# A new order for the steps of 32 batches of Performer attention, head attention and eight experts on one Trainium2 core: pieces of the same tile shape put side by side

## The chip, the cores and the metric
One core of one Trainium2 chip. The time is the device time of one launch in microseconds. Of the kernel before, three runs gave 1332.08, 1335.20 and 1335.43 us; their median, 1335.2 us, is what the changed kernel is held against.

## What is computed
For each of 32 batches, 256 tokens of width 256 (all float32):

```
x = x + tanh(g_xattn) * performer(layernorm(x), ctx, ctx, features)   # 16 heads of 16, 64 features, causal
x = x + tanh(g_ffn) * ffn(layernorm(x))

performer: q, k scaled; q' = exp(q@F) + 1e-4, k' = exp(h_k + k@F - max h_k) + 1e-4
           running sums S += k' v, Z += k'; out = (q' S) / (q' Z)
ffn:       h = rmsnorm(x); q = h@Wq + bq; k, v = ((h@Wdown + bdown)@Wup + bup)
           att = softmax over the 16 heads of one token of q k / 4; out = att v
           x = x + out@Wo + bo
           h2 = rmsnorm(x); gate = softmax(h2@Wg + bg)
           x + sum over 8 experts of gate_e * (h2 @ We_e)
```

## The kernel before
The five engines run hand-written streams in one block, synchronised by semaphores. Every step of a batch is a small function under `@per_batch`, which issues it once for each batch and in order. Each engine has a written-out start (some fifty to a hundred and twenty steps) and then `for n in range(-1, NB + 3): slot(n)`; `slot(n)` is the engine's fixed order in the steady part, and a step's argument (`n - 3` to `n + 1`) is the batch that it works on in this slot. So five batches are in flight. Before its instructions a step waits for the steps of other engines that it needs (`wait_ge(*at("name", batch))`); these waits hold for some ranges of batches only, where an earlier wait of the same engine doesn't already cover them. `Signal` groups steps of an engine on one semaphore, so steps of one group have to come in the order of the group. Eight banks of PSUM are given to the steps by hand in `BANK`.

TensorE's steps, in order of the mathematics, with their tile shapes and, for one batch, the matmul records of the trace (each has one weight load; plain float32 products count twice):

- `keys_turned`, `queries_turned`, `h_tr_`: transposes of the context, of the normed x and of the key norms. 128x128; 4, 4 and 2.
- `fk_`, `fq_`: the random features of keys and queries, rows of 32 (`feature_products`, L1609 and L1616). 20 and 12.
- `X00_`, `X01_`, `X10_`, `X11_`: scores of the first 128 keys against all queries, and `Y0_`, `Y1_`: of the second 128 keys against the second 128 queries. Rows of 64 (L1624, L1632). 8 each and 16 each. ScalarE or VectorE copies them to `att`, GpSimd or VectorE masks them.
- `av0_` to `av3_`: attended values, columns of 32 (L1639). 16 each. `nt_t_` turns the numerators (L1649). 8.
- `hn_turned`, `dn_`, `qq_`, `kv0_`, `kv1_`: the layer-normed x turned, and the projections of the second block. 128x128; 4, 6, 12, 2, 2.
- `s0_` to `s3_`: the head scores of each token, in four pieces (`head_scores`, L1658); `pv0_` to `pv3_`: the head mix, in four pieces (`head_mix`, L1666). Tiles of 32x32, 64 matmuls of 16 columns and 64 loads in each piece. These eight pieces are 512 of a batch's 792 matmuls.
- `o_tr_`, `out_project`, `h2_t0_`, `h2_t1_`, `g_`, `g_t_`: the head output turned, its projection, the second norm turned, the gate. 128x128 but for `g_t_`, which has rows of 8; 4, 12, 2, 2, 6, 2.
- `mm00_` to `mm03_`, `mm10_` to `mm13_`: the experts, two at a time, for the two halves of the tokens (`expert_products`, L1593 to L1595). 128x128, six matmuls of 512 columns each. VectorE adds each result to `z`, weighted by the gate (`a00_` and so on, L1047).

Between `pv3_` and `o_tr_` stand VectorE's `out_tokens` (L1056) and GpSimd's `out_normal` (L395). TensorE's steady order before is:

```
mm01 hn mm02 X00 dn o_tr qq X01 mm03 kv0 c_tr kv1 h_tr o Y0 s0 X10 av0 s1 av1 X11 s2 Y1 mm10
h2_t0 s3 av2 h2_t1 mm11 x_tr av3 fk nt_t g mm12 g_t pv0 fq pv1 mm13 pv2 mm00 pv3
```

(`c_tr` is `keys_turned`, `x_tr` `queries_turned`, `hn` `hn_turned`, `o` `out_project`.) A dense piece is issued like this:

```python
for n in range(32 * part // PARTS, 32 * (part + 1) // PARTS):
    for j in range(4):
        r = slice(32 * j, 32 * j + 32)
        last = pe.matmul(ps[r, BANK["pv"], n:512:32], p_t[r, n, :], v_t[r, :, n],
                         start=True, stop=True, tile_position=(32 * j, 32 * j))
```

Of the kernel before, what the change touches and what calls it, by code (L numbers as in the profile page):

```python
# [5 lines left out]
F32 = mybir.dt.float32  # L6
# [73 lines left out]
def build(nc, x_d, ctx_d, gx_d, gf_d, rf_d, g1_d, wq_d, bq_d, wdn_d, bdn_d, wup_d, bup_d,  # L80
          wo_d, bo_d, g2_d, wg_d, bg_d, we_d, out_d):
    ctx = ExitStack()
    with ctx:
# [94 lines left out]
        with ExitStack() as early:  # L178
# [30 lines left out]
            signal("q_pe", "c_t"),  # L209
            signal("q_pe_b", "h_tr"),  # L210
# [3 lines left out]
            signal("q_dve_c", "k_lo q_lo"),  # L214
            signal("q_act", "h_hi h_t_"),
            signal("q_act_b", "k_hi"),
            signal("q_act_c", "xn q_hi"),
            signal("q_pool", "rstd q_r"),
            signal("r0_pe", "fk fq"),
            signal("r0_act", "ek2 eq3"),  # L220
            signal("r0_act_b", "ek1 eq0 eq2"),
            signal("r0_act_c", "ek3"),
            signal("r0_act_d", "ek0 eq1"),
            signal("r0_pool", "pk2 pk3"),
            signal("r0_pool_b", "pq0 pq3"),
            signal("r0_pool_c", "pk1 pq1 pq2"),
            signal("r0_pool_d", "pk0"),
            signal("p0_pe", "X00 X01 Y0 av0 av1"),
            signal("p0_dve", "y00"),
            signal("p0_dve_b", "y01"),  # L230
            signal("p0_act", "x000 x011 nt0"),
            signal("p0_act_b", "x001 x010"),
            signal("p0_pool", "v1"),
            signal("p0_pool_b", "m00 m01"),
# [3 lines left out]
            signal("p1_act", "x100 x111 nt1"),  # L238
            signal("p1_act_b", "x110"),
            signal("p1_act_c", "x101"),  # L240
            signal("p1_pool", "m10 m11 x1"),
            signal("g_dve", "g_st g_mv g_bn"),
            signal("g_act", "hn y"),
            signal("g_pool", "r_f g_r yb"),
            signal("f_pe", "h_t dn qq kv0 kv1 s3"),
            signal("f_dve", "ht_lo d_lo bqq q_t bkv1 k_t v_t p_t s_sum s_tok ssum"),
            signal("f_dve_b", "bkv0 smax ssub"),
            signal("f_act", "ht_hi d_hi q_bd p_bd s_exp"),
            signal("o_pe", "pv3"),
            signal("o_pe_b", "o_tr o h2_t0 h2_t1"),  # L250
            signal("o_dve", "o_tok ot_lo y2 h2_lo0 h2_lo1"),
            signal("o_act", "ot_hi sq h2n h2_hi0 h2_hi1"),
            signal("o_pool", "o_n ms_e r2"),
            signal("o_pool_b", "z_y z0"),
            signal("e_pe", "g g_t mm00"),
            signal("e_pe_b", "mm01 mm02 mm03 mm10 mm11 mm12 mm13"),
            signal("e_dve", "ga gmax gm gsum grec gate a00_ a00"),
            signal("e_dve_b", "a01_ a01 a02_ a02 a03_ a03 a10_ a10 a11_ a11 a12_ a12 a13_ a13"),
# [31 lines left out]
        def _(sp):  # L290
            @per_batch
            def load_x_(q):
                if 2 <= q <= 4:
                    sp.wait_ge(*at("x1", q - 2))
                sp.dma_start(x_in[q % 2][:, :, :], rows(x_d, q)).then_inc(*x_load.up(q))
# [39 lines left out]
            for n in range(-1, NB + 3):  # L335
                slot(n)
# [6 lines left out]
        def _(pool):  # L343
# [3 lines left out]
            @per_batch  # L347
            def pk2_(q):
                if q in (0, 1) or q >= 3:
                    pool.wait_ge(*at("ek2", q))  # L350
                pool.tensor_scalar(pairs(kf, q, 2), pairs(kf, q, 2), KERNEL_EPS, 1.0, ALU.add, ALU.mult).then_inc(*up("pk2", q))

            @per_batch
            def values(p):
                if not p:
                    pool.wait_ge(*w_dve.at("v1_one"))
                pool.tensor_copy(v1[:, :, :, 0:HD], c_in[p % 2][:, :, :].rearrange("p t (h d) -> p t h d", d=HD)).then_inc(*up("v1", p))

            @per_batch
            def g_r_(g):  # L360
                pool.wait_ge(*at("g_bn", g))
# [7 lines left out]
            @per_batch  # L369
            def pq0_(q):  # L370
                if q in (0,) or q >= 3:
                    pool.wait_ge(*at("eq0", q))
                pool.tensor_scalar(pairs(qf, q, 0), pairs(qf, q, 0), KERNEL_EPS, 1.0, ALU.add, ALU.mult).then_inc(*up("pq0", q))  # L373

            @per_batch
            def pk1_(q):
                if q in (0, 2):
                    pool.wait_ge(*at("ek1", q))
                pool.tensor_scalar(pairs(kf, q, 1), pairs(kf, q, 1), KERNEL_EPS, 1.0, ALU.add, ALU.mult).then_inc(*up("pk1", q))

            @per_batch
            def pk0_(q):
                if q <= 1:
                    pool.wait_ge(*at("ek0", q))
                pool.tensor_scalar(pairs(kf, q, 0), pairs(kf, q, 0), KERNEL_EPS, 1.0, ALU.add, ALU.mult).then_inc(*up("pk0", q))

            @per_batch
            def pq1_(q):
                pool.wait_ge(*at("eq1", q))
                pool.tensor_scalar(pairs(qf, q, 1), pairs(qf, q, 1), KERNEL_EPS, 1.0, ALU.add, ALU.mult).then_inc(*up("pq1", q))  # L390
# [7 lines left out]
            @per_batch  # L398
            def pk3_(q):
                if not q:  # L400
                    pool.wait_ge(*at("ek3", q))
                pool.tensor_scalar(pairs(kf, q, 3), pairs(kf, q, 3), KERNEL_EPS, 1.0, ALU.add, ALU.mult).then_inc(*up("pk3", q))

            @per_batch
            def pq3_(q):
                if q <= 2:
                    pool.wait_ge(*at("eq3", q))
                pool.tensor_scalar(pairs(qf, q, 3), pairs(qf, q, 3), KERNEL_EPS, 1.0, ALU.add, ALU.mult).then_inc(*up("pq3", q))

            @per_batch  # L410
            def pq2_(q):
                if q in (0,) or q >= 2:
                    pool.wait_ge(*at("eq2", q))
                pool.tensor_scalar(pairs(qf, q, 2), pairs(qf, q, 2), KERNEL_EPS, 1.0, ALU.add, ALU.mult).then_inc(*up("pq2", q))

            @per_batch
            def m00_(p):
                if not p:
                    pool.wait_ge(*at("x000", p))
                if p:  # L420
                    pool.wait_ge(*at("x010", p))
                pool.affine_select(out=att[:, 0, :, 0:P], in_=att[:, 0, :, 0:P], compare_op=ALU.is_ge, fill=0.0, base=0,
                                   pattern=[[0, 4], [1, P]], channel_multiplier=-1).then_inc(*up("m00", p))

            @per_batch
            def m01_(p):
                if p <= 1:
                    pool.wait_ge(*at("x011", p))
# [1711 lines left out]
```

## Time and profile before

| | |
|---|---|
| runs | 1332.08, 1335.20, 1335.43 us; median 1335.2 |
| profiled execution | 1344.52 us |
| its span | 1342.8 us, 55815 instructions |
| mean granted clock of TensorE in it | 0.982 of 2.4 GHz |
| busy: TensorE, VectorE, ScalarE, GpSimd | 93%, 70%, 56%, 42% |

The profiled execution is one run by itself, so shares and durations are compared within it. TensorE's row counts matmuls; its weight loads run beside them and have a row of their own, `PEld`. In the waits and in the chain "issue" is time in which an engine stood and no semaphore explains it. The granted clock is 1.00 at 2.4 GHz and 0.50 at 1.2 GHz.

### The profile page before, as it was taken

The numbers are of one execution on the slowest core, as the hardware profiler recorded it, in microseconds if no ns is written. First come the engines' busy times: TensorE is split into PE (matmuls) and PEld (weight loads), VectorE is DVE, ScalarE is ACT, GpSimd is POOL, SyncE is SP. The second block draws the span as 40 slices with busy tenths as digits, with TensorE's granted clock in tenths as the row PEclk, the third lists the DMA queues.
The fourth block names the chain that finished last, engine by engine and source line by source line (L and its number), as shares of the span: only waits on it lengthen the run. The fifth ranks groups of instructions, "written<-read, shape, count | busy, mean of one in ns | idle before, by whom it ended". The sixth has DMA issues, their size and how long they took to land.

```text
span 1342.8 us, 55815 instructions
## 1 busy us (share of the span) xinstructions
PE 1255.5 (93%) x25344; PEld 975.1 (73%) x25344; DVE 936.9 (70%) x2166; ACT 755.1 (56%) x1502; POOL 559.2 (42%) x873
## 2 busy tenths in 40 slices
PE   0568999999999999999999999999999999999997
PEld 0347777777777777777777777777777777777775
DVE  5465677677777677766777777777777777777665
ACT  5366655565555565654556556555665555566431
POOL 0254345343434443443444444454444434444421
PEclk9987999999999999998999999999999999999999
DMA  8300000000000000000000000000000000000000
GB/s 283 106 18 18 19 26 26 27 3 26 27 26 26 27 18 11 26 27 26 26 27 8 21 26 27 26 26 27 26 2 27 26 26 26 27 26 3 10 19 16
DMA packets 40221, 40.72 MB, mean 30 GB/s; under 512 B 4144, under 2 KB 39728, under 8 KB 39984
## 3 DMA queue, kind: packets, MB, share of 16 engines
q1 hardware_dynamic: 38896, 37.11, 8.9%
q8 instruction: 199, 3.26, 1.0%
q14 instruction: 38, 0.31, 0.1%
q10 hardware_dynamic: 1088, 0.04, 0.1%
HBM read 28.75 MB, written 8.39 MB: 28 GB/s over the span
## 4 chain that ended last, share of the span: by engine, by line
PE 92%; DVE 3%; issue 2%; POOL 1%; DMA 1%; SPq 1%; ACT 1%; DVEq 0%
PE ps L1593 15%; PE ps L1595 12%; PE ps L1594 12%; PE ps L1624 10%; PE ps L1639 8%; PE ps L1666 7%; PE ps L1658 6%; PE ps L1632 5%; PE ps L1587 4%; PE ps L1609 4%; PE ps L1649 3%; DVE hk L1367 1%; PE ps L1875 1%; DMA x_in<-in_x 1%; SPq L319 1%
## 5 line engine op out<-in xcount | busy, mean ns | idle before, releaser
L1047 DVE SCALAR_TENSOR_TENSOR z<-ps,gate,z 128x256 f32<-128x256 f32 x512 | 247.4, 483 | 143.8 <-PE ps L1595 133.3
L1593 PE MATMUL ps<-we_hi,h_hi 128*128 128x512 f32 x512 | 226.2, 442 | 3.3 <-issue 1.2
L1595 PE MATMUL ps<-we_hi,h_lo 128*128 128x512 f32 x512 | 204.9, 400 | 0.0
L1594 PE MATMUL ps<-we_lo,h_hi 128*128 128x512 f32 x512 | 204.1, 399 | 0.0
L1624 PE MATMUL ps<-qf,kf 64*128 64x256 f32 x1024 | 148.9, 410 | 4.0 <-POOL qf L373 4.0
L1593 PEld LDWEIGHTS ps<-we_hi,h_hi 128*128 128x128 f32 x512 | 97.6, 191 | 33.4 <-issue 12.2
L1666 PEld LDWEIGHTS ps<-v_t,p_t 32*32 32x32 f32 x8192 | 84.3, 107 | 48.7 <-issue 47.8
L495 POOL TENSOR_TENSOR x<-o_x,x_in 128x512 f32<-128x512 f32 x32 | 41.1, 1285 | 188.3 <-DVE o_x L1274 188.3
L1624 PEld LDWEIGHTS ps<-qf,kf 64*128 64x128 f32 x1024 | 90.5, 190 | 34.4 <-issue 23.0
L1595 PEld LDWEIGHTS ps<-we_hi,h_lo 128*128 128x128 f32 x512 | 97.9, 191 | 23.2
L1639 PE MATMUL ps<-att,v 128*32 128x256 f32 (+1 forms) x2048 | 111.9, 334 | 1.2 <-DVE att L1205 0.6
L1666 PE MATMUL ps<-v_t,p_t 32*32 32x16 f32 x8192 | 98.8, 186 | 13.2 <-issue 13.1
L1594 PEld LDWEIGHTS ps<-we_lo,h_hi 128*128 128x128 f32 x512 | 98.4, 192 | 12.4 <-issue 0.3
L1658 PEld LDWEIGHTS ps<-k_t,q_bd 32*32 32x32 f32 x8192 | 81.3, 105 | 28.5 <-issue 23.4
L435 POOL TENSOR_SCALAR ms_e<-ms 128x2 f32<-128x2 f32 x32 | 6.1, 191 | 227.5 <-ACT h2n L696 227.5
L1658 PE MATMUL ps<-k_t,q_bd 32*32 32x16 f32 x8192 | 94.3, 185 | 2.8 <-issue 2.0
L1196 DVE TENSOR_TENSOR att<-ps,causal 128x512 f32<-128x512 f32 x32 | 22.1, 691 | 97.0 <-PE ps L1632 97.0
L1639 PEld LDWEIGHTS ps<-att,v 128*32 128x32 f32 x2048 | 54.8, 109 | 43.0 <-issue 17.7
L615 ACT ACTIVATE ht_hi<-ps 128x512 fp32r<-128x512 f32 x32 | 19.2, 599 | 116.5 <-PE ps L1587 116.5
L659 ACT ACTIVATE q_bd<-q_t,sel_tok 128x512 f32<-128x512 f32 x64 | 76.6, 1254 | 2.7 <-DVE q_t L1113 2.7
L395 POOL TENSOR_TENSOR o_n<-o_tok,s_rec 128x512 f32<-128x512 f32 x32 | 41.6, 1300 | 85.6 <-DVE o_tok L1056 85.5
L1632 PE MATMUL ps<-qf,kf 64*128 64x128 f32 x1024 | 74.9, 284 | 1.3 <-issue 1.2
(210 smaller groups left out, 3076.4 us busy)
## 6 DMA issues: line engine op xcount, KB each, us to landing
x_in<-in_x SPq DMA_DIRECT2D x32, 256.0 KB, 3.5
c_in<-in_ctx SPq DMA_DIRECT2D x32, 256.0 KB, 3.2
c_chunk<-in_ctx SPq DMA_DIRECT2D x16, 512.0 KB, 7.4
out<-z SPq DMA_DIRECT2D x32, 256.0 KB, 2.6
stage<-in_L_ffn_We SPq DMA_DIRECT2D x2, 1024.0 KB, 9.8
stage_q<-in_L_ffn_Wq SPq DMA_DIRECT2D x1, 256.0 KB, 6.4
stage_u<-in_L_ffn_Wup SPq DMA_DIRECT2D x2, 128.0 KB, 5.4
stage_b<-in_L_ffn_bup SPq DMA_DIRECT2D x1, 256.0 KB, 6.6
```

The lines of the kernel that those rows point to most:

```text
L659: last = act.activation(q_bd[:, :, t, :], q_t[:, :, :].rearrange("p h n -> p n h"), ACT.Copy, scale=sel_tok[:, t:t + 1])
L1047: return dve.scalar_tensor_tensor(out=z[e % 2][:, t, :], in0=ps[:, bank, ex % 2 * D:(ex % 2 + 1) * D], scalar=gate[:, t, ex:ex + 1], in1=z ...
L1587: last = pe.transpose(out[:, c * L + t * P:c * L + (t + 1) * P], src[:, t, c * P:(c + 1) * P], ident[:, :])
L1593: pe.matmul(out, a_hi(c), b_hi(c), start=(c == 0), stop=False)
L1594: pe.matmul(out, a_hi(c), b_lo(c), start=False, stop=False)
L1595: last = pe.matmul(out, a_lo(c), b_hi(c), start=False, stop=(c == C - 1))
L1609: last = pe.matmul(ps[:, BANK[f"f{of}{r}"], :], weight[own, :], src[own, :, :].rearrange("p c l -> p (c l)"), start=(n == 0), stop=(n == 2 ...
L1624: last = pe.matmul(ps[:, banks[half], j * L:(j + 1) * L], kf[b % 2][r, pr, 0:P], qf[b % 2][r, pr, :], start=True, stop=True)
L1632: last = pe.matmul(ps[:, banks[half], j * P:(j + 1) * P], kf[b % 2][r, pr, P:L], qf[b % 2][r, pr, P:L], start=True, stop=True)
L1639: last = pe.matmul(ps[32 * j:32 * j + 32, bank, half * L + part * P:half * L + L], v1[:, part, 8 * oct + 2 * j + half, :], att[:, half, j, ...
L1658: last = pe.matmul(ps[r, BANK["s"], n * H:(n + 1) * H], q_bd[r, n, :, :], k_t[r, :, n], start=True, stop=True, tile_position=(32 * j, 32 * j))
L1666: last = pe.matmul(ps[r, BANK["pv"], n:512:32], p_t[r, n, :], v_t[r, :, n], start=True, stop=True, tile_position=(32 * j, 32 * j))
```

## The change
Every step keeps its instructions. What changes is their place, for all engines: the order in the slots, the waits that go with it, the grouping of steps on semaphores, the banks, the written-out start (161 steps instead of 86 on TensorE), and how far batches are apart in one slot. The slots now run from -2, and the first products of a batch stand one slot earlier (`n + 1` instead of `n`), its keys and queries too (`n + 2` instead of `n + 1`); the experts run over `n - 3` and `n - 2`.

```diff
-BANK = dict(x000=5, x001=0, x010=0, x011=3, y00=7, y01=4, av0=7, x100=6, x101=2, x110=5, x111=4, y10=7, y11=6,
-            av1=0, fq0=3, fq1=4, fq2=0, fq3=1, fk0=5, fk1=4, fk2=7, fk3=6, c=0, h=3, x=1, nd0=0, nd1=3, ht=3,
-            dn=3, qq=5, kv0=7, kv1=1, s=1, pv=6, otr=7, o=5, h20=5, h21=2, g=2, mm00=7, mm01=2, mm02=1,
-            mm03=6, mm10=3, mm11=3, mm12=7, mm13=2)
+BANK = dict(x000=3, x001=7, x010=5, x011=0, y00=6, y01=5, av0=2, x100=6, x101=5, x110=0, x111=1, y10=3, y11=2,
+            av1=4, fq0=4, fq1=6, fq2=3, fq3=1, fk0=1, fk1=5, fk2=6, fk3=2, c=5, h=0, x=3, nd0=2, nd1=5, ht=7,
+            dn=4, qq=7, kv0=2, kv1=3, s=7, pv=4, otr=0, o=7, h20=2, h21=1, g=2, mm00=0, mm01=0, mm02=4,
+            mm03=3, mm10=6, mm11=1, mm12=3, mm13=6)
...
             def slot(n):
-                load_x_(n + 1)
-                load_c_(n + 1)
+                load_x_(n + 2)
+                load_c_(n + 2)
                 write(n - 3)
```

TensorE's steady order after the change (pairs of pieces side by side are joined by `+`; the batch of each step in brackets, relative to n):

```
mm10(-3) mm11(-3) g(-2) X00+X01(+1) pv0+pv1(-1) Y0(+1) h_tr(+2) g_t(-2) mm12(-3) hn(0)
av0+av1(+1) X10+X11(+1) pv2+pv3(-1) Y1(+1) mm13(-3) c_tr(+2) o_tr(-1) x_tr(+2) dn(0) qq(0)
fk(+2) av2+av3(+1) kv0+kv1(0) o(-1) mm00(-2) nt_t(+1) fq(+2) s0+s1(0) mm01(-2) mm02(-2)
s2+s3(0) h2_t0(-1) h2_t1(-1) mm03(-2)
```

In the start the order is its own; there the first pieces stand as `s0+s1 fq s2+s3`, `pv0+pv1 av0 av1 X10 pv2+pv3`, and for batches 1 and 2 `pv0+pv1+pv2`. VectorE's slot after the change, for the chains that the text speaks of:

```
g_bn(0) p_turned(-1) a10(-3) h_lo(+2) a11(-3) y01(+1) gate_bias(-2) y00(+1) ssum(-1) q_bn(+2)
gate_max(-2) a12(-3) out_tokens(-1) y11(+1) y10(+1) ht_low(0) a13(-3) k_low(+2) gate_weights(-2)
d_lo(0) bqq(0) q_low(+2) ot_low(-1) q_turned(0) bkv1(0) bkv0(0) second_sum(-1) k_turned(0)
a00(-2) v_turned(0) den(+1) numerators_over(+1) a01(-2) a02(-2) smax(0) ssub(0) h2_lo1(-1)
h2_lo0(-1) a03(-2)
```

## Rows read from the trace of the kernel before

**Rows 1.** The page: busy time of the engines, and the chain that ended last

```profile
PE 1255.5 (93%) x25344; PEld 975.1 (73%) x25344; DVE 936.9 (70%) x2166; ACT 755.1 (56%) x1502; POOL 559.2 (42%) x873
...
PE 92%; DVE 3%; issue 2%; POOL 1%; DMA 1%; SPq 1%; ACT 1%; DVEq 0%
```

**Rows 2.** The waits of TensorE: us in total, times, longest us

```profile
PE ps L1666 <- issue: 13.1, 14, 2.0
...
PE ps L1587 <- ACT hn L609: 6.3, 1, 6.3
...
PE ps L1658 <- issue: 2.0, 1, 2.0
PE ps L1632 <- issue: 1.2, 3, 0.5
PE ps L1593 <- issue: 1.2, 2, 0.7
```

**Rows 3.** The chain, one batch apart: start us, us, what (`Y1_`)

```profile
522.46 1.09 PE ps L1632 x16
...
560.73 1.09 PE ps L1632 x16
```

**Rows 4.** The chain: one head piece, the expert product behind it, two head pieces

```profile
535.84 0.67 PE ps L1666 x64
536.51 0.43 PE ps L1593
536.94 0.23 PE ps L1594
...
1274.56 1.20 PE ps L1666 x121
```

**Rows 5.** The timeline of TensorE at the end: start us, us; three head pieces

```profile
1292.08 1.80 PE L1658 MATMUL ps<-k_t,q_bd 32*32 32x16 f32 x192 [0.82 <-DVE k_t L1141]
```

**Rows 6.** The chain: two attention pieces, `Y1_` behind `X11_`, one attention piece

```profile
61.13 1.44 PE ps L1639 x32
...
63.63 0.92 PE ps L1632 x16
...
529.00 0.79 PE ps L1639 x16
```

**Rows 7.** The page: the DMA queue that fetches instructions; packets, MB, share

```profile
q8 instruction: 199, 3.26, 1.0%
```

**Rows 8.** The timeline of TensorE in the start, waits in brackets

```profile
95.01 0.60 PE L1632 MATMUL ps<-qf,kf 64*128 64x128 f32 x5 [0.51 <-issue]
95.53 1.22 PE L1658 MATMUL ps<-k_t,q_bd 32*32 32x16 f32 x123
98.74 0.25 PE L1658 MATMUL ps<-k_t,q_bd 32*32 32x16 f32 x5 [1.98 <-issue]
...
112.69 1.36 PE L1666 MATMUL ps<-v_t,p_t 32*32 32x16 f32 x83 [1.99 <-issue]
```

**Rows 9.** The timeline of TensorE in the steady part: issue waits

```profile
259.64 0.32 PE L1666 MATMUL ps<-v_t,p_t 32*32 32x16 f32 x16 [0.98 <-issue]
...
615.35 0.42 PE L1666 MATMUL ps<-v_t,p_t 32*32 32x16 f32 x17 [1.27 <-issue]
...
657.30 0.57 PE L1666 MATMUL ps<-v_t,p_t 32*32 32x16 f32 x45 [1.11 <-issue]
...
1122.66 0.24 PE L1666 MATMUL ps<-v_t,p_t 32*32 32x16 f32 x3 [1.04 <-issue]
```

**Rows 10.** Windows: length, busy PE, PEld, DVE, ACT, POOL; PEclk, DMA, GB/s

```profile
614.80:621.60 6.80, 6.25 (x92) 4.75 (x92) 1.58 (x7) 2.77 (x6) 3.99 (x8) 0.50 0.15 45
...
1123.40:1126.80 3.40, 3.40 (x70) 2.43 (x69) 1.34 (x5) 1.60 (x4) 3.00 (x6) 0.50 0.02 5
```

**Rows 11.** The timelines of VectorE and of GpSimd: the head output

```profile
542.60 0.65 DVE L1056 STREAM_TRANSPOSE o_tok<-ps 128x512 f32<-128x512 f32 x1
...
543.34 1.30 POOL L395 TENSOR_TENSOR o_n<-o_tok,s_rec 128x512 f32<-128x512 f32 x1 [1.66 <-DVE o_tok L1056]
```

More of the change, by code:

```diff
@@ L410, in pq2_ @@
[L410 to L423, printed above, removed]
@@ new lines, in _ @@
+            pq2_(3)
+            pk2_(3)
+            attended(2)
+            g_r_(2)
+            m00_(3)
+            m01_(3)
+            q_r_(4)
+            out_normal(1)
+            m10_(3)
+            m11_(3)
+            yb_(1)
+            pk0_(4)
+            pq1_(4)
+            second_scale(1)
+            z0_(1)
+            pk1_(4)
+            pq3_(4)
+            pq2_(4)
+            attended(3)
+            pk2_(4)
+            pq0_(4)
+            pk3_(4)
+            g_r_(3)
@@ L590, in _ @@
+            m01_(4)
+            values(4)
+            m00_(4)
+            q_r_(5)
+            yb_(2)
+            out_normal(2)
+            m11_(4)
+            m10_(4)
+            z0_(2)
+            second_scale(2)
+            pk3_(5)
+            pk2_(5)
+            pq2_(5)
+            attended(4)
+            pq0_(5)
+            pk1_(5)
+            pk0_(5)
+            pq1_(5)
+            pq3_(5)
+            yb_(3)
+            for n in range(-2, NB + 3):
                 slot(n)
@@ new lines, in _ @@
+            h_rows(4)
+            x100_(3)
+            nt0_(3)
+            ht_high(2)
+            x110_(3)
+            x_normal(4)
+            d_hi_(2)
+            ot_high(1)
+            x101_(3)
+            x111_(3)
+            h_hi_(5)
+            q_high(4)
+            k_high(4)
+            nt1_(3)
+            q_apart(2)
+            ek2_(4)
+            ek0_(4)
+            ek3_(4)
+            ek1_(4)
+            eq1_(4)
+            sq_(1)
+            eq2_(4)
+            eq0_(4)
@@ new lines, in _ @@
+            second_normal(1)
+            eq3_(4)
+            h2_hi1_(1)
+            y_normal(2)
+            h2_hi0_(1)
+            p_apart(2)
+            x000_(4)
+            x001_(4)
+            gate_logits(1)
+            x010_(4)
+            x011_(4)
+            weights_exp(2)
+            h_normal(3)
+            h_rows(5)
+            x_normal(5)
+            ht_high(3)
+            nt0_(4)
+            x110_(4)
+            x101_(4)
+            x111_(4)
+            d_hi_(3)
+            ot_high(2)
@@ new lines, in _ @@
+            x100_(4)
+            k_high(5)
+            gexp_(1)
+            q_high(5)
+            q_apart(3)
+            ek2_(5)
+            ek0_(5)
+            nt1_(4)
+            ek1_(5)
+            ek3_(5)
+            eq0_(5)
+            sq_(2)
+            eq1_(5)
+            second_normal(2)
+            eq2_(5)
+            eq3_(5)
+            y_normal(3)
+            h2_hi1_(2)
+            h2_hi0_(2)
+            p_apart(3)
+            weights_exp(3)
+            for n in range(-2, NB + 3):
@@ new lines, in X11_, with pv2_, pv3_, Y1_ @@
+            def X11_(p):
+                if p + 1 < NB:
+                    pe.wait_ge(*at("h_t_", p + 1))
+                first_keys(p, 1, 1, BANK["x110"], BANK["x111"]).then_inc(*up("X11", p))
+            @per_batch
+            def pv2_(f):
+                head_mix(2)
+            @per_batch
+            def pv3_(f):
+                head_mix(3).then_inc(*up("pv3", f))
+            @per_batch
+            def Y1_(p):
+                if p >= 4:
+                    pe.wait_ge(*at("a12", p - 4))
+                pe.wait_ge(*at("nt0", p))
+                second_keys(p, 1, BANK["y10"], BANK["y11"]).then_inc(*up("Y1", p))
```

2096 lines of the change are left out of this document (1166 added, 930 removed).

## The prediction

> **What bounds the kernel now.** Read the page first: TensorE is busy 93% of the span and the chain that ended last is 92% TensorE; VectorE is busy 70%, ScalarE 56%, GpSimd 42% [rows 1]. So the sum is one over TensorE's own stream, and the other engines matter only where TensorE would wait for them. The waits say how little it does: past the start-up hardly any wait for another engine is left, but "issue", time in which nothing that the profile shows holds TensorE back, comes to 13.1 + 2.0 + 1.2 + 1.2 = 17.5 us, 13.1 of it in one line, the second product of the head attention [rows 2]. One batch takes 560.73 - 522.46 = 38.3 us where nothing disturbs it [rows 3]; 32 of them are 1225 us.
>
> Two costs lie in that stream besides the products.
>
> First, **a price on each change of tile shape**. A 128x128 product of 512 columns takes 0.23 us in the chain behind its like, and 0.43 behind a 32x32 piece [rows 4]: 0.20 more. A piece of 64 head products takes 0.67 alone and two side by side 1.20 [rows 4], 0.14 less than twice the one; three side by side 1.80 [rows 5], 0.10 less for each of the further two. I take 0.12, between them. An attention piece (`av`) takes 0.79 alone and 1.44 for two, 0.14 saved; the second-keys product takes 1.09 alone and 0.92 behind the first-keys product of its own shape, 0.17 saved [rows 3, 6].
>
> Second, **the instructions have to be fetched**. The fetching queue moved 3.26 MB in 199 packets [rows 7], 16 KB each; over 50,688 loads and products [rows 1] that is 255 instructions for each packet. At 95.01 TensorE resumes from an issue wait, runs 5 + 123 products with as many loads, exactly 256 instructions, and stands 1.98 us until 98.74 [rows 8]: a packet takes 3.7 us there, though the instructions in it took 1.8. At 112.69, in the one place where the four pieces of the head mix stand side by side, it has stood 1.99 us again [rows 8]. In the steady part the waits over 0.8 us number seven, of 0.84 to 1.27 us, all in the head mix (four of them, the first, the longest and the last among them: [rows 9]): there 256 instructions hold two pieces (0.67 each) and one short step between (0.9 to 1.6), some 2.1 to 2.9 us.
>
> Behind such waits **TensorE's clock falls**. The wait at 615.35 lies beside a stretch of 6.8 us at a granted clock of 0.50, so 1.2 GHz, and the one at 1122.66 right before 3.4 us of it [rows 9, 10]; of the seven waits five are followed by such a fall, four of 3.4 us and this one of 6.8, 20.4 us together, while the wait of 1.11 us at 657.30 has none.
>
> **The change, part by part.**
> Nothing is computed differently, so the products' number stands. Counting through both orders by their shapes, a steady batch goes from 29 changes of shape to 19: into 128x128 from 8 to 6, into 32x32 from 8 to 4, into 64-row from 6 to 4, into 32-column from 4 to 2, the rest equal. Of the 64-row kind I take 0.19, since a 128x128 step after it shows 0.20. Over the whole order with its written-out start it is 909 to 604: 63, 120, 64 and 60 fewer, two more of the 32-row kind. 63 x 0.20 + 120 x 0.12 + 64 x 0.19 + 60 x 0.14 = 12.6 + 14.4 + 12.2 + 8.4 = 47.6, **-48 us**. For `X01` behind `X00` and `X11` behind `X10` no clean row exists; between nothing and 0.20 I take the same 0.19 by its nearest kin, `Y` behind `X` [rows 6]. At nothing the term is 12 us smaller.
>
> The fetch gets worse. Before, the eight dense pieces stood apart; now four pairs of 256 instructions take 1.2 us each [rows 4]. A packet that coincides with a pair leaves 3.7 - 1.2 = 2.5 us to wait; one that takes in neighbours waits less, and the wait is gone when these have lasted 2.5 us. An expert product gives 1.6 us to 12 instructions (19 instructions for 2.5 us), the first-keys products 1.06 to 16 (about 38), the second-keys product 1.09 to 32 and then an expert product or other short steps (about 40). Where packets begin drifts from batch to batch, since a batch is no multiple of 256. So the odds of a wait: pair `pv0,pv1` and pair `pv2,pv3` (38 + 40)/256 each, pair `s0,s1` (38 + 19)/256, pair `s2,s3` (19 + 20)/256, together 0.99 a batch, of 1.25 us on average: 37 us in 30 batches. Against 17.5 now, **+19 us**. Bounds: 0 if the neighbours (12 to 36 instructions in 2 to 3 us, which stand where dense pieces stood) were enough, and +43 if a packet takes 4.4 us.
>
> The clock: of thirty waits spread evenly up to 2.5 us two thirds, 20, are over 0.8. By five in seven that would be 14 falls; I take 13, since the pairs of the scores now stand beside expert products, at the 4.1 us (20.4 / 5) of now: 53 us at half clock against 20.4. TensorE is busy all through such a stretch [rows 10], so near half of such a stretch is lost, 0.47: **+15 us** (25 - 9.6), bounds 0 and +30.
>
> Waits for other engines, by hand along the new order: the tightest is the head output. `pv3` ends, then `Y1` 1.09, `mm13` 1.59 and the key transposes 0.44 run, and 3.1 us later `o_tr` wants `o_n`. That is `o_tok` 0.65 and `o_n` 1.30 with 0.1 between each [rows 11], 2.1 to 2.2, if VectorE is free. An accumulation pair (1.0) or the softmax sum (1.2) in front uses up the 0.9 left. The other chains have more: from the layer norm of the attended batch to `hn` there are now over 18 us where 10.7 stood; from `s3` to `pv0` 7.9 against 8.2. I take **+2 us**, bounds 0 and +30. Banks are only renamed; each bank's next writer stands behind a wait that by the same hand count is met with 0.7 us or more. The x and context loads are issued a slot earlier on SP (slot n+2 against n+1) ahead of the same store; they land in about 3 us and the queue has time. Between masks and adds GpSimd keeps its 17.5 us a batch. None of these is on the path.
>
> Start and end: the 6.3 us wait for `hn` [rows 2] gets the whole of batch 1's first products in front of it, but these wait themselves for the features' exponentials and adds, and ScalarE's expert weights now stand ahead of `nt0`. At the end the last batch's output chain has fewer steps to hide behind. Both signs, some 4 us each way: **0**.
>
> **Sum:** -48 + 19 + 15 + 2 = **-12 us**, against the profiled execution's 1344.5 (span 1342.8): 1332.5 there. The median of the runs is 1335.2, 9.3 lower; the difference is carried over: **1323 us**.
>
> **Rivals.**
> 1. *The fetch takes it all back* (slower). Place: the four pairs. It decides once fetch and clock together cost 46 us more. For: side by side the pieces stood 2 us each time [rows 8], and a packet that takes 4.4 us makes 61 us of waits (+43) and 20 falls (+28). Against: the drift of packets spares most batches. -48 + 43 + 28 + 2 = +25: about 1360. A milder mix lies at 1340. Chance 0.14.
> 2. *The short steps between are enough.* Then waits stay near 18 us and the clock where it is: -48 + 2 = -46, 1289; with half of both terms 1306. For: the pair at 1274.56 ran through [rows 4]. Against: the two long waits [rows 8]. Chance 0.2. The Trainium skill, "Runtime: NRT & Kernel Launch", section "Instruction fetch mechanics", would go this way: it gives TensorE's instruction memory as 2048 instructions and calls the fetch hidden by the rate of issue. By that rule no pair could wait. The trace speaks against it with its waits every 256 instructions.
> 3. *A wait for `o_n`* in each batch, 1 us x 31 batches, takes the place of the saving: -12 + 31 - 2 = +17, 1352. The 0.9 us left speaks against. Chance 0.05.
> 4. *The price is not one of changing shape* but of each piece's first load, so only a third of the 48 us comes: -16 + 36 = +20, 1355. Against: it shows in three kinds of steps [rows 4 to 6]. Chance 0.04.
>
> **How the numbers follow.** The forecast, 1310 to 1335, has 0.57, rival 2 0.2, the slow ones 0.23. About 0.3%, 4 us, is what a measurement of this kernel can tell from no change. Faster: rival 2 and nearly all of the forecast, 0.73. Same (1331 to 1339): 0.11. Slower: 0.16. Range: down to half of rival 2's terms, up past no change to where one slow case in two lies: 1300 to 1342.
>
> **What would show it.** A batch in 36.7 us where undisturbed (2 x 0.20 + 4 x 0.12 + 2 x 0.19 + 2 x 0.14 = 1.5 less than 38.3, within 0.2); two pieces of head products in 1.2 us throughout; issue waits of 30 to 45 us in all, in `s1`, `s2`, `pv1`, `pv3` and what follows them, up to 2.5 us long; 12 to 18 stretches at half clock. Wrong would be: an undisturbed batch at 38 us, issue waits under 20 us (rival 2) or over 55 (rival 1), or a wait for GpSimd's `o_n` in each batch (rival 3).

## The result, and the profile after

The changed kernel takes **1278.1 us** (median of 4 runs, 1275.15 to 1283.31) against 1335.3 us for the kernel before on the same chip: a ratio of 0.958, 95% interval 0.954 to 0.962. The forecast was 1323, with 1300 to 1342 as its range. The direction was right and the gain came out nearly five times as large: 57 us instead of 12.

The page of the changed kernel, in the lines that answer to [rows 1, 7]:

```profile
span 1281.4 us, 55870 instructions
...
PE 1200.8 (94%) x25344; PEld 980.0 (76%) x25344; DVE 934.2 (73%) x2166; ACT 741.4 (58%) x1502; POOL 560.4 (44%) x873
...
PEclk9988889999999999999999999999999999999999
...
q8 instruction: 199, 3.26, 1.1%
...
PE 92%; DVE 3%; issue 2%; ACT 1%; POOL 1%; DMA 1%; ACTq 0%; DVEq 0%
```

The same products, the same 199 packets, 61.4 us less span, and the chain is 92% TensorE as before. The waits of TensorE, which answer to [rows 2] (columns as there):

```profile
PE ps L1858 <- POOL qf L453: 7.1, 2, 4.7
PE ps L1900 <- issue: 5.5, 4, 2.2
...
PE ps L1892 <- issue: 3.3, 5, 1.3
...
PE ps L1843 <- issue: 1.2, 1, 1.2
PE ps L1821 <- POOL o_n L420: 1.2, 2, 0.6
```

L1892 and L1900 are the two products of the head attention. The issue waits were to grow; they shrank, from 18.0 us over the whole execution to 13.3. The waits for `o_n` are two, none of them in the steady part.

The timeline of TensorE (as in [rows 8]) at `X00_` of two batches with nothing in between that disturbs, and then the one place of the steady part at which the clock still fell, with the window around it (columns of [rows 10]):

```profile
810.16 2.00 PE L1858 MATMUL ps<-qf,kf 64*128 64x256 f32 x16
...
846.66 2.00 PE L1858 MATMUL ps<-qf,kf 64*128 64x256 f32 x16
```

```profile
613.30 1.22 PE L1892 MATMUL ps<-k_t,q_bd 32*32 32x16 f32 x122
615.52 0.25 PE L1892 MATMUL ps<-k_t,q_bd 32*32 32x16 f32 x6 [1.00 <-issue]
...
616.60:620.00 3.40, 3.40 (x10) 2.40 (x8) 0.97 (x2) 0.00 (x0) 3.08 (x5) 0.51 0.34 86
```

A batch takes 846.66 - 810.16 = 36.50 us against 38.27 between the two rows of [rows 3]: 1.77 less, where 1.54 was forecast. The chain holds the new groups at the lengths the prediction gave them:

```profile
403.89 0.12 PE ps L1829
404.00 1.93 PE ps L1858 x16
405.93 1.20 PE ps L1900 x123
407.13 1.12 PE ps L1866 x16
408.25 0.37 PE ps L1980 x2
408.62 0.22 PE ps L1988 x2
408.84 0.43 PE ps L1827
409.27 0.23 PE ps L1828
...
410.86 1.44 PE ps L1873 x32
412.30 1.93 PE ps L1858 x16
```

`X00_` and `X01_` side by side take 1.93 (1.06 and then 0.86), two head pieces 1.20, two attention pieces 1.44.

Where the time went, by stretches of the two profiled executions. "Steady" runs from `X00_` of batch 5 to that of batch 31, 26 batches. "Half clock" is the time at a granted clock of 0.50. Everything is counted up to TensorE's last instruction.

| | before | after |
|---|---|---|
| first instruction to `X00_` of batch 5 | 227.7 us | 219.7 |
| steady | 1020.0 | 957.3 |
| from there to TensorE's last instruction | 91.3 | 100.6 (`X00_` stands a stage earlier, so more is left to do) |
| issue waits: start, steady, end | 6.0, 11.3, 0.6 | 8.7, 4.0, 0.6 |
| half clock: start, steady, end | 23.9, 20.5, 3.4 | 30.7, 3.4, 6.8 |
| waits for other engines, in all | 65.4 | 63.5 |

The steady part has lost 62.7 us. 26 x 1.77 = 46.0 is the undisturbed batch; the issue waits gave 7.3, and 17.1 us less at half clock, in which TensorE gets near half done, about 8.5: together 61.8. So three quarters of the gain are the changes of tile shape, as forecast, and a quarter is the fetch and the clock, which were to cost 34 us and gave back 16. Each column is one execution, and the one of before took 1344.5 us at a mean granted clock of 0.982, where 19 later runs of that kernel have a median of 1336.4 us, at 0.986: it spent more time at half clock than is usual, so the share of the clock is put too high here.

The question for the runs was therefore twofold. Is the order's gain really the price of changes of shape? And why does the fetch, which stood at each of [rows 8, 9] in front of less dense code, hardly show in the new order?

### The profile page after: what moved, and what is told of

It is laid out like the page before. It is cut to its first block, busy times and chain, and to the rows that moved or that the text cites. A ratio compares the mean times of both kernels' runs of the same rounds, so it can differ in the third digit from the quotient of the medians.

```text
span 1281.4 us, 55870 instructions
## 1 busy us (share of the span) xinstructions
PE 1200.8 (94%) x25344; PEld 980.0 (76%) x25344; DVE 934.2 (73%) x2166; ACT 741.4 (58%) x1502; POOL 560.4 (44%) x873
## 4 chain that ended last, share of the span: by engine, by line
PE 92%; DVE 3%; issue 2%; ACT 1%; POOL 1%; DMA 1%; ACTq 0%; DVEq 0%
PE ps L1827 14%; PE ps L1829 13%; PE ps L1828 13%; PE ps L1858 10%; PE ps L1873 7%; PE ps L1900 6%; PE ps L1892 6%; PE ps L1866 6%; PE ps L1821 4%; PE ps L1843 4%; PE ps L1883 2%; PE ps L2139 1%; PE ps L1980 1%; DVE hk L1534 1%; PE ps L2241 1%
## 5 line engine op out<-in xcount | busy, mean ns | idle before, releaser
L1827 PE MATMUL ps<-we_hi,h_hi 128*128 128x512 f32 x512 | 215.4, 421 | 2.5 <-DVE z L1191 2.5
L1858 PE MATMUL ps<-qf,kf 64*128 64x256 f32 x1024 | 136.0, 406 | 9.5 <-POOL qf L453 7.1
L1858 PEld LDWEIGHTS ps<-qf,kf 64*128 64x128 f32 x1024 | 98.4, 196 | 31.2 <-issue 15.5
L438 POOL TENSOR_SCALAR z<-y,tanh_f 128x512 f32<-128x512 f32 x32 | 22.3, 697 | 213.0 <-DVE y L1423 213.0
L1827 PEld LDWEIGHTS ps<-we_hi,h_hi 128*128 128x128 f32 x512 | 96.8, 189 | 23.9 <-DVE z L1191 3.3
L1873 PE MATMUL ps<-att,v 128*32 128x256 f32 (+1 forms) x2048 | 99.8, 336 | 2.4 <-DVE att L1263 1.2
L1900 PEld LDWEIGHTS ps<-v_t,p_t 32*32 32x32 f32 x8192 | 76.0, 105 | 27.8 <-issue 26.2
L1892 PEld LDWEIGHTS ps<-k_t,q_bd 32*32 32x32 f32 x8192 | 75.7, 104 | 26.1 <-issue 15.3
L1900 PE MATMUL ps<-v_t,p_t 32*32 32x16 f32 x8192 | 83.0, 185 | 6.6 <-issue 5.5
L1892 PE MATMUL ps<-k_t,q_bd 32*32 32x16 f32 x8192 | 82.7, 184 | 3.8 <-issue 3.3
L714 ACT ACTIVATE nt<-ps 128x512 f32<-128x512 f32 x32 | 19.1, 597 | 94.2 <-PE ps L1873 94.2
L1315 DVE STREAM_TRANSPOSE o_tok<-ps 128x512 f32<-128x512 f32 x32 | 23.0, 718 | 68.4 <-PE ps L1900 68.4
L1866 PEld LDWEIGHTS ps<-qf,kf 64*128 64x128 f32 x1024 | 65.6, 194 | 6.7 <-ACT att L685 4.1
L510 POOL TENSOR_TENSOR y<-y,b_o 128x512 f32<-128x512 f32 x32 | 41.3, 1292 | 52.7 <-ACT y L890 52.7
```

What stands on the lines that cost most here:

```text
L1827: pe.matmul(out, a_hi(c), b_hi(c), start=(c == 0), stop=False)
L1858: last = pe.matmul(ps[:, banks[half], j * L:(j + 1) * L], kf[b % 2][r, pr, 0:P], qf[b % 2][r, pr, :], start=True, stop=True)
L1866: last = pe.matmul(ps[:, banks[half], j * P:(j + 1) * P], kf[b % 2][r, pr, P:L], qf[b % 2][r, pr, P:L], start=True, stop=True)
L1873: last = pe.matmul(ps[32 * j:32 * j + 32, bank, half * L + part * P:half * L + L], v1[:, part, 8 * oct + 2 * j + half, :], att[:, half, j, ...
L1892: last = pe.matmul(ps[r, BANK["s"], n * H:(n + 1) * H], q_bd[r, n, :, :], k_t[r, :, n], start=True, stop=True, tile_position=(32 * j, 32 * j))
```

## Experiments

Each was run in 3 rounds against the kernel before on the same chip; "steady" is from here on a profiled execution's stretch from 200 us to 75 us before its end (11.8 us of issue waits in the kernel before and 4.4 in the changed one; 20.5 and 3.4 us at half clock). Only orders, and in e10 to e14 a wait or ScalarE's order, are changed; everything is computed in all of them.

**The price of a change of shape: e1 and e4.** e1 pulls the four score pieces apart again, e4 the first pair of the first-keys products:

```diff
 e1                          e4
-s0_ s1_ mm01_ mm02_        -g_ X00_ X01_
-s2_ s3_ h2_t0_ h2_t1_      +X00_ g_ X01_
+s0_ mm01_ s1_ mm02_
+s2_ h2_t0_ s3_ h2_t1_
```

> The changed kernel with its score pieces taken apart on TensorE in the steady slots: s0 mm01 s1 mm02 s2 h2_t0 s3 h2_t1 in place of s0 s1 mm01 mm02 s2 s3 h2_t0 h2_t1; four changes of shape more in a batch, two into 32x32 and two into 128x128, nothing else moved. Theory 1 (each change of shape has its price): 2 x 0.12 + 2 x 0.20 = 0.64 us a batch over some 30 batches, +19 us against the changed kernel's 1278, so about 1297, and an undisturbed batch of 37.1 against 36.5. Rival (the gain came from the new stage distances, and the sides of a piece are nearly free): under +5 us. For the fetch: pieces apart should have no more issue waits than the changed kernel has (4 us from 200 us on).

> The changed kernel with the gate product between the two first-keys products (X00 g X01 in place of g X00 X01): one change into the 64-row shape and one into 128x128 more in a batch, no dense piece touched. Theory 1: 0.20 + 0.20 = 0.4 us a batch, +12 us, 1290, with X00 then 1.06, g 0.91 and X01 1.06 in the chain where g 0.71 and X01 0.86 stood. Rival (that step was the one without a clean row before; a 64-row product behind its own kind gains nothing): +6 us or less.

e1 took 1295.7 us (ratio 0.970, 0.967 to 0.974), e4 1289.8 (0.966, 0.963 to 0.969). An undisturbed batch takes 37.13 us in e1 and 36.86 in e4, so 0.63 and 0.36 more than 36.50; by the prices (two into 128x128 and two into 32x32, 0.64; one into 64-row and one into 128x128, 0.39) it was to be 0.64 and 0.39. Both are within 0.03 us. e1's issue waits in the steady part are 6.6 us, so standing apart didn't help the fetch. **The price is that of changing shape**, and it adds up.

**How close may dense pieces stand: e2 and e3.** All four score pieces together, or two pairs with one expert product between instead of two:

```diff
 e2                              e3
-s0_ s1_ mm01_ mm02_ s2_ s3_    -s0_ s1_ mm01_ mm02_ s2_ s3_
+s0_ s1_ s2_ s3_ mm01_ mm02_    +s0_ s1_ mm01_ s2_ s3_ mm02_
```

> The changed kernel with all four score pieces side by side (s0 s1 s2 s3 mm01 mm02): two changes of shape fewer in a batch, but 512 instructions of the dense kind with nothing between. By the price of shapes alone it gains 2 changes, 0.32 us a batch, -10 us: 1268. Theory 2 (a packet of 256 instructions is asked for ahead of need, by the time of the few dozen instructions that the sequencer is ahead of the array; two packets in a row in 2.2 us can't be covered by that): an issue wait of 1.5 to 2.5 us in nearly every batch, 50 to 70 us in all, and the clock falls behind most of them (30 or more stretches of 3.4 us), together +80 us or more: 1350 to 1380. Rival (the fetch no longer matters in the changed kernel): about 1268, issue waits under 15 us.

> The changed kernel with one expert product between the two score pairs in place of two (s0 s1 mm01 s2 s3 mm02): as many changes of shape, the same dense pairs, only 1.6 us and 12 instructions between them where 3.0 us and 24 were. Price of shapes alone: 1278. Theory 2 (asked for ahead of need): one product hides part of the second packet: short issue waits of 0.3 to 0.8 us in many batches, 12 to 30 us in all, hardly more clock falls, total +8 to +25 us: 1286 to 1303. The rule of my prediction (a packet is asked for when the one before begins to run on the array) would have given the changed kernel 37 us of waits and this one some 50.

e2 took 1390.3 us (ratio 1.039, 1.035 to 1.044), e3 1319.3 (0.987, 0.984 to 0.991), both above the range that was expected. The waits of TensorE in e2:

```profile
PE ps L1892 <- issue: 62.0, 32, 2.7
PE ps L1900 <- DVE p_t L1212: 7.3, 24, 1.9
```

and in e3:

```profile
PE ps L1892 <- issue: 19.5, 29, 1.8
PE ps L1900 <- DVE p_t L1212: 7.3, 23, 2.1
```

Here is rival 1, in full: with four pieces in a row there is one wait in every batch, of 1.9 us on average, 119.5 us of the steady part run at half clock, and two changes of shape fewer are worth nothing beside it. With one expert product (1.4 to 1.6 us) between the pairs each batch still waits 0.7 us; with two, 0.1. So the fetch of [rows 8] is real, and what the changed order has is just enough room. e3's span is 37.3 us longer than the changed kernel's: 17 us are issue waits of the steady part, about 5 the clock (10 us more at half), 6 the wait for `p_t`, which I hadn't costed; the other 9 or so I didn't follow up. That wait has its cause on VectorE, which adds `mm02`'s product in front of the row maxima: with `mm02` after `s3` the softmax would start later by this order, and `pv0` waits 0.2 us in nearly each batch; the order of VectorE wasn't varied.

**Order alone, at the old stage distances: e5 and e9.** Is it the order that gains, or the new banks and distances? e5 gives the kernel before the pairs of the head mix, e9 these and all others that its distances allow (705 changes of shape against 909 and 604):

```diff
 e5                                   e9, besides
-pv0_ fq_ pv1_ mm13_ pv2_ mm00_ pv3_ -Y0_ s0_ X10_ av0_ s1_ av1_ X11_
+pv0_ pv1_ fq_ mm13_ mm00_ pv2_ pv3_ -s2_ Y1_ mm10_ h2_t0_ s3_ av2_
                                     +Y0_ X10_ s0_ s1_ av0_ av1_ X11_
                                     +Y1_ mm10_ s2_ s3_ h2_t0_ av2_
```

> The kernel before with its old stage distances and banks, and the head mix alone in the new manner: pv0 pv1 side by side, then fq, mm13, mm00, then pv2 pv3 (before: each of the four apart by one short step). Changes of shape go from 909 to 821 (30 fewer into 128x128, 58 fewer into 32x32): by the prices 30 x 0.20 + 58 x 0.12 = 13 us less. Theory (a packet is requested well before its first instruction is used, so three short steps between two pairs hide it): the issue waits of the steady part, 11.8 us before, fall to some 5 us, and its half clock from 20 us to under 10, together about 10 us more: 1312 us, ratio 0.983. Rival (the gain came from the new stage distances, the pairs cost what they save): 1335 or slower, issue waits over 15 us. The prices alone, without a change in waits: 1322.

> The kernel before with its old stage distances and banks, its TensorE slot put in pairs as far as those distances let it: X10, s0 s1, av0 av1, X11, Y1, mm10, s2 s3, then h2_t0, av2, h2_t1, mm11, and the head mix as in e5. Changes of shape from 909 to 705: 1 x 0.20 + 58 x 0.19 + 116 x 0.12 + 29 x 0.14 = 29 us less by the prices. Theory (order alone makes the gain, the stage distances only make room for it): issue waits of the steady part some 5 us, half clock under 10, so another 10 us: 1296 us, ratio 0.970, plus whatever waits for VectorE or ScalarE the moved pieces bring (the steady part has none before), which the distances of the changed kernel would have kept off. Rival (the new distances and banks make the gain): over 1325 without any new wait for another engine in the steady part.

Both expectations failed. e5 took 1330.6 us (ratio 0.997, 0.994 to 1.000), e9 **1342.2** (1.005, 1.003 to 1.007): slower than before, with 204 changes of shape fewer. The shapes saved about what was priced (an undisturbed batch of 37.65 us in e9 is 0.62 less, 0.9 without a new wait of `Y1_` for ScalarE's `nt`, 0.27 in each batch; by the prices 1.0), but issue waits of the steady part rose to 16.4 us in e5 and 21.1 in e9, and half clock to 34.1 and 37.5. The changed kernel has pairs too, and 4.4 and 3.4. Between the pairs of the head mix e9 has three short steps in 3.8 us; the changed kernel has only two expert products in 3.0 between its score pairs and waits less there. Distance alone couldn't be it.

**When the packet is asked for.** Windows of the changed kernel (columns as in [rows 10]) around `s0` `s1` of batch 14 and of batch 27, in which no other transfer runs:

```profile
611.70:612.90 1.20, 1.20 (x16) 0.99 (x17) 1.16 (x3) 0.21 (x2) 1.12 (x2) 1.00 0.00 0
612.90:614.10 1.20, 1.20 (x106) 0.85 (x101) 1.12 (x6) 0.67 (x2) 1.03 (x3) 1.00 0.06 14
614.10:615.50 1.40, 0.42 (x50) 0.32 (x39) 0.88 (x2) 1.40 (x4) 1.24 (x3) 1.00 0.00 0
1091.10:1092.30 1.20, 1.20 (x11) 0.98 (x9) 1.09 (x3) 0.78 (x4) 1.12 (x2) 1.00 0.06 14
1092.30:1093.50 1.20, 1.20 (x41) 0.73 (x43) 1.17 (x6) 0.10 (x1) 1.05 (x2) 1.00 0.00 0
1093.50:1094.70 1.20, 1.20 (x125) 1.17 (x113) 1.13 (x5) 1.20 (x3) 1.09 (x2) 1.00 0.00 0
```

14 GB/s over 1.2 us are the 16 KB of one packet. That the issue waits are waits for such packets can be counted: in all 15 traces those behind 200 us (245, of over 0.15 us) end 2.2 to 3.0 us after a packet's transfer began, and by a count of TensorE's loads, products and semaphore instructions every one of them falls on the same place of a step of 256, within two instructions. In batch 14 the packet comes while the array is about to begin `s0` (613.30), and the array stands until 615.52, 2.6 us after the transfer began. In batch 27 the transfer begins at 1091.1, over 2 us ahead of `s0` (1093.27), while the array is in a few long instructions, and 125 products then run in 1.2 us without a stop. The edge between two steps of 256 lies at the same place in both pairs, 122 and 123 products in. So what counts is how far ahead of the dense code the request goes out. Who sends it?

**A wait met just in time: e12, e11, e14.** The timelines of ScalarE and TensorE in the kernel before, ahead of `pv0`:

```profile
610.43 0.37 ACT L780 ACTIVATE gl<-ps 8x256 f32<-8x256 f32 x1 [0.64 <-PE ps L1595]
610.71 0.57 ACT L786 ACTIVATE kf<-ps 128x512 f32<-128x512 f32 x1
...
611.92 0.47 PE L1666 MATMUL ps<-v_t,p_t 32*32 32x16 f32 x34
```

`pv0` waits for the key feature `ek3` (L786), whose bank it takes over. That is done at 611.28, 0.64 us before `pv0` starts, in every batch. The array loses nothing by it, and no view of waits shows it. But TensorE's sequencer, which goes ahead of the array, has to stop at this wait: the view of that line has it passing there at 611.3, as soon as `ek3` is done.

```profile
L1945 PEldq EVENT_SEMAPHORE  x1: 51/51/51, 611.3 to 611.3; - x1
```

Its lead over the array is 0.56 us then, and if it is the sequencer that asks for the next packet, the packet is asked for late, right in front of the densest code. In the changed kernel `ek3` is off this path. The edit takes one line of ScalarE's order, and TensorE's isn't touched; e12 is the kernel before with it, e11 is e9 with it:

```diff
                 ek1_(n + 1)
+                ek3_(n + 1)
                 gate_logits(n - 2)
-                ek3_(n + 1)
```

> The kernel before, with ScalarE's ek3 moved ahead of the gate logits' copy and nothing else. Theory: as in e11, in the old order; issue waits of the steady part from 11.8 us to 6 to 9 and half clock from 20.5 to under 12, 1329 us (1325 to 1333). Rival: no effect, 1335 within 3.

> The kernel before with its slot in pairs (as e9), and one edit besides: ScalarE computes the fourth key feature (ek3) ahead of the copy of the gate logits instead of behind it. pv0 waits for ek3, since pv and that feature share a bank; the sequencer passes that wait 0.56 us before pv0 starts, and with the edit it would 1.5 us before. TensorE's order is the same as in e9. Theory (the late-met wait in front of pv0 costs the lead of the fetch): issue waits of the steady part fall from 21.1 us to 10 to 15, half clock from 37.5 us to under 20, so 1342 falls to 1328 (1320 to 1334). Rival (the wait for ek3 doesn't matter, the pairs as such are too close): issue waits 18 to 24, 1340 or more.

e12 took 1331.1 us (ratio 0.997, 0.995 to 0.999; the kernel before beside it 1336.4), with 4.5 us of issue waits in the steady part and no half clock where 11.8 and 20.5 stood. The profiled executions overstate this: their spans are 16.5 us apart, the medians 5.3, since the one of before is a slow one. By the median granted clocks of all runs (0.986 and 0.988) the edit saves some 5 us at half clock, an estimate. e11 took 1332.9 against e9's 1342.2, with issue waits of 17.6 us for 21.1 and 30.7 us at half clock for 37.5. So the effect is there, but in e11 only the time came out within what was expected; the waits (10 to 15) and the half clock (under 20) stayed near those of the rival. Its timelines say why:

```profile
722.25 0.61 ACT L786 ACTIVATE kf<-ps 128x512 f32<-128x512 f32 x1
723.00 0.37 ACT L780 ACTIVATE gl<-ps 8x256 f32<-8x256 f32 x1
...
724.49 0.50 PE L1666 MATMUL ps<-v_t,p_t 32*32 32x16 f32 x37
```

`ek3` is done 1.63 us ahead now, but `g_t`, which stands in front of `pv0`, waits for the gate logits (L780), done at 723.37, 1.12 ahead. In the trace the sequencer passes `pv0`'s wait 1.02 us before `pv0`, where it was 0.56 in e9. e14 takes that away too: the gate products `g` go ahead of `nt_t`, their like in shape (with the waits that `g` then needs, met 1.7 us ahead).

```diff
-                nt_t_(n)
                 g_(n - 2)
+                nt_t_(n)
```

> e11 (the kernel before in pairs, ek3 earlier) with the gate products g moved ahead of the numerators' transposes, its like in shape, so that ScalarE's copy of the gate logits is done earlier too; in e11 this copy was done 1.12 us before pv0, and g_t in front of pv0 waits for it. No change of shape more or less. The last late wait ahead of pv0 is then met some 1.5 us before it (e9: 0.56, e11: 1.02). Theory: issue waits of the steady part from 17.6 us to 12 to 16, half clock from 30.7 to under 28, 1327 us (1318 to 1332). Rival (what is left in e11 comes only from the pairs standing 3.8 us apart, where the changed kernel has 7): 1333 within 3, issue waits 16 to 20.

```profile
713.66 0.36 ACT L780 ACTIVATE gl<-ps 8x256 f32<-8x256 f32 x1
...
715.47 0.51 PE L1666 MATMUL ps<-v_t,p_t 32*32 32x16 f32 x38
```

The logits are done 1.45 us ahead, and the sequencer passes the last wait 1.35 us before `pv0`. e14 took **1315.3 us** (ratio 0.985, 0.981 to 0.989), more than was expected of it. The three kernels, with the same pairs at the same distances:

| | last wait ahead of `pv0` passed | issue waits, steady | half clock, steady | time |
|---|---|---|---|---|
| e9 | 0.56 us before it | 21.1 us | 37.5 us | 1342.2 us |
| e11 | 1.02 | 17.6 | 30.7 | 1332.9 |
| e14 | 1.35 | 9.7 | 6.8 | 1315.3 |

Not one of these waits held the array. 27 us hang on 0.8 us of slack. From e9 to e11 TensorE's instructions are the same. e14 has 30 semaphore instructions more, so its steps of 256 fall elsewhere, which could be a cause of its own; but the gain is there at like places too. In e9 and e11 nine steps end at the 93rd product of the pair `pv0` `pv1` or later, and the array waits 1.5 and 1.1 us there on average; in e14 eight do, and it waits 0.4.

**The same in the changed kernel, with a control: e10 and e13.** `s0` of the changed kernel gets one wait that it doesn't need, late in e10, long met in e13:

```diff
                     pe.wait_ge(*at("q_bd", f))
+                if 6 <= f <= 29:
+                    pe.wait_ge(*at("z0", f - 1))    # e13: f - 2
                 head_scores(0)
```

> The changed kernel with one wait added in front of s0, which the computation doesn't need: for GpSimd's sum z of the batch before, which in the profile is done 0.11 us before s0 starts, in every batch. Nothing else moves. Theory (a packet of instructions is requested when TensorE's sequencer comes to it, tens of instructions ahead of the array; a wait that is met only just in time holds the sequencer back although the array loses nothing by it): the array's own start of s0 slips by no more than 0.1 us a batch, some 2 us, but where a packet boundary falls into the first part of s0 s1 its successor is requested up to 1.4 us later: issue waits in the steady part from 4.4 to 9 to 15 us, with half-clock stretches behind some, 1287 us (1282 to 1294). Rival (a wait that is met in time is free, packets go by the array's own position): issue waits stay at 4 to 6.5 us and the time within 3 us of 1278.

> The control to e10: the changed kernel with the same extra wait in front of s0, but for GpSimd's sum of one batch earlier, which has been done for over 30 us. The same number of instructions as e10, so the same places of the packet boundaries. Theory (what cost e10 its time is that the wait is met late): issue waits of the steady part 4 to 7 us against 12.3 in e10, and the time back at 1278 (1275 to 1282). Rival (one more instruction of this kind in front of s0, or the shifted boundaries, cost the time): 1286 or more, issue waits over 9 us.

e10 took 1289.3 us (ratio 0.965, 0.961 to 0.969), e13 1278.9 (0.957, 0.954 to 0.961). The undisturbed batch is 36.51 and 36.50 us, so the wait costs nothing where no packet is due. Where one is, the timelines of TensorE at the same place of the program, 123 products into `s0` and `s1` of batch 27, show e10

```profile
1097.69 1.21 PE L1892 MATMUL ps<-k_t,q_bd 32*32 32x16 f32 x123
1101.38 0.25 PE L1892 MATMUL ps<-k_t,q_bd 32*32 32x16 f32 x5 [2.48 <-issue]
```

and e13

```profile
1087.24 1.22 PE L1892 MATMUL ps<-k_t,q_bd 32*32 32x16 f32 x123
1089.15 0.24 PE L1892 MATMUL ps<-k_t,q_bd 32*32 32x16 f32 x5 [0.70 <-issue]
```

The same boundary costs 1.78 us more. At the one in batch 14 it costs the whole wait: e10 stands 2.76 us, and e13 (second) runs its 128 products in one row:

```profile
611.96 1.21 PE L1892 MATMUL ps<-k_t,q_bd 32*32 32x16 f32 x122
615.93 0.30 PE L1892 MATMUL ps<-k_t,q_bd 32*32 32x16 f32 x6 [2.76 <-issue]
```

```profile
609.22 1.27 PE L1892 MATMUL ps<-k_t,q_bd 32*32 32x16 f32 x128
```

The packets show the request itself: in batches 14, 18 and 27 their transfers begin 1.05, 1.15 and 1.06 us behind the start of `s0` in e10, and 2.12, 0.52 and 0.45 us ahead of it in e13. So **the packet is asked for later when a wait ahead of it is met late**, though the array hasn't waited there. One boundary alone proves little, since in the start, where the two run the same code, the waits at one boundary differ by up to 0.5 us, and at that of batch 14 the changed kernel itself waits 1.00. The sums stand clear: in the whole steady part issue waits are 12.3 us against 5.0, half clock 10.2 against 0, and the runs (1282.9 to 1295.4 us, and 1277.9 to 1280.2) don't overlap.

**A better order still: e7 and e8.** e7 puts `Y1_` behind `X10_ X11_` and `o_tr` behind the query transposes (577 changes), e8 also `g_t` in front of `h_tr` (551).

> The changed kernel with Y1 moved in front of pv2 pv3 (behind X10, X11, its like) and the output transposes o_tr behind the query transposes: one change into the 64-row shape fewer in each batch, 604 to 577. Theory (a change into that shape costs 0.19 us): 27 x 0.19 = 5 us less, 1273 us, if o_tr, now after mm13, keys and queries, still finds o_n ready. Rivals: the second-keys product costs the same wherever it stands (1278), or TensorE waits 0.5 us and more in each batch for o_n (1290 and more), since Y1 stood in o_n's cover.

> As e7, and besides the gate transposes g_t moved between Y0 and h_tr, beside no 128x128 product: one change of 0.20 us fewer in each batch, 551 changes in all. Theory: 5 us by e7's part and 26 x 0.20 = 5 us by this: 1268 us, ratio to the kernel before 0.950, an undisturbed batch in 36.1 us against 36.5. Rivals: leaving g_t costs the same in front of any shape, then only e7's part is left (1273); or with fewer stops TensorE stands closer to its fetches and the issue waits rise from 4.4 us by as much.

e7 took 1280.4 us (ratio 0.960, 0.957 to 0.963), e8 1276.1 (0.956, 0.952 to 0.960). In e7 `Y1_` takes 0.89 us instead of 1.09, as priced, but the query transposes, now right behind the key transposes, take 0.62 instead of 0.44, and the batch stays at 36.54. e8's undisturbed batch is 36.34, 0.20 below e7's by `g_t` alone, as priced; its issue waits in the steady part are 6.5 us. So neither brought the 5 and 10 us that were expected. By the batch e8 is a few us better than the changed kernel; the measured times don't tell them apart (the intervals overlap nearly whole). Both beat the kernel before by as much as the change does.

## Why the prediction was wrong

**Changes of shape (-48): right, slightly small.** The count of 909 to 604 stands, an undisturbed batch saved 1.77 us where 1.54 was worked out, and e1 and e4 find each price within 0.03 us. The value taken for `X01_` behind `X00_` without a clean row, 0.19, was 0.20 (0.86 against 1.06). Expert products behind their like took 1.36 to 1.38 instead of 1.39, under 0.1 us of the 0.23 that a batch saved beyond the forecast; the rest wasn't followed up. Rival 4 is out.

**Fetch (+19): this step failed.** Measured, the whole execution has 4.7 us less in issue waits (18.0 to 13.3), not 19 more. The odds and the excess were worked out as if a packet were due from the moment at which the array enters 256 instructions (3.7 us, by the wait at 98.74 of [rows 8]), so that a packet which coincides with a pair of 1.2 us had to be waited for, whatever stood in front of it. The sequencer is ahead of the array: with the short steps in front (12 instructions in 1.6 us, 16 in 1.0) it comes to the next boundary earlier, and the request goes out earlier with it, over 2 us ahead of `s0` in the window at 1091.1. The places of [rows 8] were no fair sample: at 112.69 four pieces stand together, and e2 is that case in each batch and has 62 us of waits; at 98.74 the array had come out of a wait only 256 instructions before (95.01). The step also read the old waits [rows 9] as the cost of two pieces with one short step between. They were mostly the cost of the late `ek3`: e12 leaves the order of TensorE as it is and has 4.5 us of them instead of 11.8, with no half clock in the steady part of its profiled execution. The new order had something to remove that the trace showed nowhere as a wait.

**Clock (+15): failed with it.** The rule by which it was worked out (a wait of over 0.8 us, then 3.4 us or more at half clock for five in seven) holds only in part. e2 has 32 waits in the scores and 119.5 us at half clock, 3.7 for each, but its waits are near twice as long as those of [rows 9]. Of waits over 0.8 us e14 has seven with 6.8 us at half clock, e1 two (1.00 and 1.13 us) with none. There were only two steady waits over 0.8 us to follow, and one fall: 3.4 us at half clock for 20.5, 8.5 us gained where 15 were to be lost. The start went the forecast way, from 23.9 to 30.7 us, three us lost.

**Waits for other engines (+2): right within 4 us**, 65.4 to 63.5. The tight one, `o_n`, was met in each steady batch: rival 3 didn't come. Where an order has no such slack e3 shows it, with `p_t`.

**Start and end (0): off by some 8 us.** Of the 305 changes saved, 45 lie outside the 26 steady batches, some 7 us by their prices; yet start and end together are 1.3 us longer (-8.0 and +9.3). The half clock there (10.2 us more, about 5) and the issue waits (2.7) explain nearly all of it.

**The rivals.** Rival 2, that the short steps between are enough, is what happened, and went further than its own 1289, since it kept the old waits. It had 0.2; I gave the two long waits [rows 8] too much weight. But the rule that I cited beside it isn't why: the Trainium skill, "Runtime: NRT & Kernel Launch", section "Instruction fetch mechanics", calls the fetch hidden by the rate of issue, with 2048 instructions held, and e2's 62 us stand against it. Rival 1's mechanism is real too, and one step away in the order: e3 gives back 41 us of the 57.

The forecast's parts as they came out, in us:

| | forecast | measured in the profiled executions |
|---|---|---|
| changes of shape | -48 | -46 in 26 batches, and some 7 outside |
| fetch | +19 | -4.7 |
| clock | +15 | -8.5 steady (against a slow execution of before), +5 outside |
| other engines | +2 | -2 |
| sum | -12 | -61.4 (spans), -57.2 (medians) |

What stays open: e9 and its kin say that late waits decide much, e2 and e3 that distance does; how many instructions the sequencer can be ahead wasn't measured by itself. Nor was it tried whether the changed kernel's own latest wait ahead of a pair (`p_t`, done 0.7 to 1.4 us before `pv0`) still costs something; of the 5.5 us of issue waits in L1900 all but 0.6 lie in the start, so in the steady part it has little to give.

## What to carry to other kernels

Where an engine runs dense code of short instructions, count two things that no list of waits shows: how much time the steps in front and between give to how few instructions, and when the last semaphore in front is met. A wait met 0.5 us ahead of dense code costs nothing in the array and may cost 2 us in the fetch, and the clock after it; moving one producer on another engine can be worth more than reordering the dense engine. And before a wait of the old trace is carried over to the new order as a cost, find out what makes it: take away its cause in the old order alone.

## What the runs showed of the hardware

- The fetch of TensorE's instructions stalls it at steps of 256 instructions although the queue is busy 1% of the time: up to 2.7 us in e2, 2.8 in e10, 3.4 in the start of e9 (L1666). The stalls end 2.2 to 3.0 us after a packet's transfer began (245 waits in 15 traces).
- A semaphore wait that is already met when the array arrives isn't free: 0.15 us of slack against over 30 us of slack cost 10.5 us of time over 24 batches (e10, e13), with up to 2.8 us at one boundary.
- That holds for a wait on a step further in front as well: `g_t`'s wait for the gate logits held back the fetch for `pv0` (e11, e14).
- Two sets of four 128x128 transposes side by side took 0.44 and 0.62 us where they took 0.44 each with another set between (e7); why wasn't looked into.
